# Messages of a graph network as three one-pass matmuls in place of fp32 ones, and h by graphs written by ScalarE and VectorE in place of GpSimd

## The chip, the cores and the metric

The kernel runs on one core of a Trainium2 chip. The metric is the device time of the program in microseconds. The engines of the core (TensorE or PE, VectorE or DVE, ScalarE or ACT, GpSimd or POOL, SyncE or SP) each run their own list of instructions and wait for one another through semaphores.

## The reference

64 graphs of 128 nodes, 128 features per node, all fp32. Each layer input x is normalised and rectified to h; a residual is added at the end.

```python
def _L0_gnn_ref(x, mask, ...):           # x is h here
    xc = jnp.transpose(x, (0, 2, 1))
    h = relu(bn1(conv1d(xc, conv1_w)))                     # 1 tap
    h = bn2(conv1d(h, conv2_w, pad=8))                     # 17 taps
    x_conv = jnp.transpose(relu(h + xc), (0, 2, 1))
    s = x @ w_se.T + b_se                                  # 3 numbers per node
    sq = jnp.sum(s * s, axis=-1)
    dist = sq[:, :, None] + sq[:, None, :] - 2.0 * jnp.einsum('bnd,bmd->bnm', s, s)
    A = jnp.exp(-dist) * mask
    msg = relu(x @ w_msg.T + b_msg)
    x_nmp = jnp.einsum('bnm,bmd->bnd', A, msg)
    gi = concatenate([x_conv, x_nmp], -1) @ w_ih.T + b_ih
    gh = x @ w_hh.T + b_hh
    r = sigmoid(gi_r + gh_r); z = sigmoid(gi_z + gh_z)
    nn_ = tanh(gi_n + r * gh_n)
    return (1.0 - z) * nn_ + z * x
h = jnp.maximum(_layernorm(x, axis=-1), 0.0)
x = x + _L0_gnn_ref(h, adj, ...)
```

The change is about `s` and `msg`: both are products of h with one weight matrix of 132 columns (128 for the messages, 3 for s, one of padding).

## The kernel before

The work goes in 8 groups of 8 graphs (`NG`, `GB`). Features lie on the 128 partitions, and a group's 1024 nodes in two halves of 512 columns (`c` = 0, 1), each in one PSUM bank. In the column order a node comes first and the graph second, so that the 8 graphs of one node are neighbours. Most products are made in three matmuls: a number is split into a high part of type F32R (rounded when written) and the rest as a low part, and `three` (L867 to L870) adds high weights by high data (L868), high weights by low data (L869) and low weights by high data (L870). Two products are fp32 before the change: the messages (L901) and the gather of messages by the affinities (L933). An fp32 matmul stands in the trace as two records of the line.

Per group TensorE runs, in an order written out by hand (L1040 to L1067): nine sub-convolutions (`sub_conv`, matmuls of 256 columns), between them the transposes and distances for the affinities, the gathers, and the transposes of the next group's h (`h_transpose(g + 1, 0, 6)` and `(g + 1, 1, 3)`, into banks 6 and 3); then `gates_h(g, 0)`, `conv1(g + 1)`, `gates_in(g, 0)`, `gates_h(g, 1)`, `messages(g + 1)`, `gates_in(g, 1)`. The gates write banks 3, 4, 5 and 6, so `gates_h(g, 0)` first waits until the next group's h has been read out of banks 6 and 3 (L968).

That reading out: ScalarE writes `h_hi` and `hf`, the high part and the full h (`h_rows`, L402 and L403); VectorE makes `h_lo` from the two (`h_low`, L627); GpSimd copies `hf` into `hg`, where each graph's nodes are together (`by_graphs`, L351), since the messages take a graph's 128 nodes as stationary operand:

```python
pool.tensor_copy(hg[:, :, c * HALF:(c + 1) * HALF],
                 hf[g % 2][:, cols(c)].rearrange("p (n b) -> p b n", b=GB)).then_inc(hg_ready, 1)
```

On VectorE the order around it is also by hand (L836 to L847): `add_shared` (L701), two `join_y` (L709, each waits for one sub-convolution), `n_low` (L729), `h_low(g + 1, 0)`, `add_shared`, `n_low`, `join_y(g, 1, 0)` (waits for sub-convolution 7), `h_low(g + 1, 1)`, `join_y(g, 1, 1)`. ScalarE then makes `xc_hi` (L483) from the finished y, after `ghn_rows` (L489), which reads the first gate matmuls.

`messages(g)` (L891): three F32R matmuls of 396, 396 and 264 columns put the bias in place (L898), then eight fp32 matmuls of 132 columns (L901), one per graph. ScalarE takes s and the messages out (L450 to L457), GpSimd makes the slots for the distances from s (`distances`, L326 to L345).

In the prologue, h and the messages of group 0 are made while the convolution weights are still being split: on ScalarE h_rows stands ahead of the bias row (L535, L536) and the weights' high parts (L385), on VectorE h_low ahead of two weight lots (L620) and the bias row's low part (L807), for which the first messages wait.

Of the kernel before, what the change touches and what calls it, by code (L numbers as in the profile page):

```python
# [10 lines left out]
P = 128  # L11
# [49 lines left out]
def gnn_kernel(nc, x_nm, x_t, adj_t, w_in, w_conv, w_gate, par_in, row_in, out):  # L61
    ctx = ExitStack()
    with ctx:
# [3 lines left out]
        def sem(name):  # L67
# [25 lines left out]

        hg = sb("hg", [P, GB, P])

# [51 lines left out]
            sem("stats_ready"), sem("mv_ready"), sem("pool_ln"), sem("rstd_ready"), sem("hn_ready"))  # L147
        ht_ps, hf_ready, hg_ready, h_lo_ready = (
            sem("ht_ps"), sem("hf_ready"), sem("hg_ready"), sem("h_lo_ready"))

# [109 lines left out]
        def _(pool):  # L260
# [85 lines left out]

            def by_graphs(g, c):
                pool.wait_ge(hf_ready, NCH * g + c + 1)

                upto(pool, msg_ps, g)  # L350
                pool.tensor_copy(hg[:, :, c * HALF:(c + 1) * HALF],  # L351
                                 hf[g % 2][:, cols(c)].rearrange("p (n b) -> p b n", b=GB)).then_inc(hg_ready, 1)

            pool.wait_ge(pool_set, 5)
            ln_scale(0)
            affine()
            by_graphs(0, 0)
            by_graphs(0, 1)
            distances(0)
            for g in range(NG):  # L360
                if g + 1 < NG:
                    ln_scale(g + 1)
                    by_graphs(g + 1, 0)
                    by_graphs(g + 1, 1)
                    distances(g + 1)

        @block.scalar
        def _(act):
# [28 lines left out]
            def h_rows(g, c, src):  # L397
                act.wait_ge(ht_ps, NCH * g + c + 1)

                upto(act, diff_ready, NCH * (g - 2) + c + 1)  # L400
                upto(act, z_ps, NCH * (g - 2) + c + 1)
                act.activation(h_hi[g % 2][:, cols(c)], bank(src), ACT.Relu)  # L402
                act.activation(hf[g % 2][:, cols(c)], bank(src), ACT.Relu).then_inc(hf_ready, 1)  # L403

            def conv1_rows(g, c, src):
# [122 lines left out]

            lot_high(0)
            ln_rows(0)  # L530
            h_rows(0, 0, 6)
# [65 lines left out]
        def _(dve):  # L597
# [25 lines left out]
            def h_low(g, c):  # L623
# [3 lines left out]
                dve.tensor_tensor(h_lo[g % 2][:, cols(c)], hf[g % 2][:, cols(c)], h_hi[g % 2][:, cols(c)],  # L627
                                  ALU.subtract).then_inc(h_lo_ready, 1)

            def level1(g):  # L630
# [164 lines left out]
            moments(0)  # L795
            lot_low(0)
            dve.wait_ge(w2_landed, 16)
            dve.tensor_tensor(fb, w2[:, 0:16:2, :], w2[:, 1:16:2, :], ALU.add).then_inc(sums_ready, 1)
            dve.wait_ge(sums_ready, 1)
            dve.tensor_tensor(fbb, fb[:, 0:8:2, :], fb[:, 1:8:2, :], ALU.add).then_inc(sums_ready, 1)  # L800
            h_low(0, 0)
            h_low(0, 1)
            lot_low(1)
            lot_low(2)
# [17 lines left out]
            for g in range(NG):  # L822
# [17 lines left out]
                if ahead:  # L840
                    h_low(g + 1, 0)
                add_shared(g, 1)
                n_low(g, 1, 7)
                join_y(g, 1, 0)
                if ahead:
                    h_low(g + 1, 1)
                join_y(g, 1, 1)  # L847
                xc_low(g, 0)
# [17 lines left out]
        def _(pe):  # L866
# [24 lines left out]
            def messages(g):  # L891
# [7 lines left out]
                for k, count in enumerate(counts):  # L899
                    for i in range(count):  # L900
                        last = pe.matmul(ps[:, k, i * MW:(i + 1) * MW], hg[:, 3 * k + i, :], w_a[:, P:P + MW],  # L901
                                         start=False, stop=i == count - 1)
                last.then_inc(msg_ps, 1)
# [59 lines left out]
            def gates_h(g, c, ahead):  # L963
                h = (h_hi[g % 2][:, cols(c)], h_lo[g % 2][:, cols(c)])
                if c == 0:

                    if ahead:
                        pe.wait_ge(hf_ready, NCH * (g + 1) + NCH)  # L968
                    else:
                        pe.wait_ge(e_ready, g + 1)  # L970
# [64 lines left out]
            conv1(0, 0, 0)  # L1035
            conv1(0, 1, 7)
            pe.wait_ge(row_split, 3)
            pe.wait_ge(row_ready, 4)
# [78 lines left out]
```

## Time and profile before

| | |
|---|---|
| median of 3 runs | 305.73 us (305.6 to 306.12) |
| profiled execution, its own time | 304.81 us |
| its span (first to last instruction) | 302.8 us |
| instructions | 5350 |
| mean granted clock of TensorE | 0.99 |
| TensorE matmuls (PE) | 279.1 us busy, 92%, 1907 records |
| TensorE weight loads (PEld) | 254.0 us busy, 84%, 1907 records |
| VectorE (DVE) | 230.5 us, 76% |
| ScalarE (ACT) | 179.4 us, 59% |
| GpSimd (POOL) | 90.5 us, 30% |
| L901, messages: matmul records | 128, 15.7 us, mean 276 ns |
| L351, hg by GpSimd | 16, 19.5 us, mean 1219 ns |

A duration is that of one instruction; matmuls overlap in the pipeline, so what a matmul costs is the distance between two starts, not its duration. The chain of waits is followed back from the last instruction, and its pieces don't overlap: a piece is the time that its work held up the end. A wait is put down to the instruction whose semaphore came last. PEclk is the granted clock as a share of 2.4 GHz. L12 is line 12 of the kernel; the changed kernel's lines differ.

### The profile page before, as it was taken

How to read it: one execution, taken by the hardware profiler on the slowest of the kernel's cores; microseconds unless marked ns; L12 is line 12 of the kernel's file. 1: busy time of each engine (PE TensorE's matmuls, PEld its weight loads, DVE VectorE, ACT ScalarE, POOL GpSimd, SP SyncE). 2: the span in 40 equal slices, each digit the busy share in tenths (PEclk: the TensorE clock that was granted, in tenths of full speed). 3: DMA queues.
4: the chain of work that ended last, by engine and by line, in shares of the span. 5: the costliest groups of instructions: out<-in, count | busy, mean ns of one | idle time of the engine just before them, and what ended most of it. 6: DMA issues, size and time to landing. Idle time of an engine off the chain costs nothing.

```text
span 302.8 us, 5350 instructions
## 1 busy us (share of the span) xinstructions
PE 279.1 (92%) x1907; PEld 254.0 (84%) x1907; DVE 230.5 (76%) x477; ACT 179.4 (59%) x342; POOL 90.5 (30%) x159
## 2 busy tenths in 40 slices
PE   0474999999999999999999999999999999999992
PEld 0254998899988998899988998899988998899892
DVE  4489976796787876796787876796787976776446
ACT  2878466657556566656566566556566576561353
POOL 4845330362205530262205520252305520220000
PEclk9998999999999999999999999999999999999998
DMA  7610030017000530017000440007000420022001
GB/s 246 228 47 1 15 128 2 0 31 246 2 3 0 145 135 1 2 19 259 2 0 2 139 141 0 4 13 247 19 0 2 140 71 0 0 61 82 2 0 69
DMA packets 6654, 18.96 MB, mean 63 GB/s; under 512 B 866, under 2 KB 1252, under 8 KB 6500
## 3 DMA queue, kind: packets, MB, share of 16 engines
q1 hardware_dynamic: 6480, 18.62, 19.0%
q8 instruction: 15, 0.25, 0.3%
q14 instruction: 11, 0.09, 0.1%
q10 hardware_dynamic: 148, 0.01, 0.0%
HBM read 14.43 MB, written 4.19 MB: 62 GB/s over the span
## 4 chain that ended last, share of the span: by engine, by line
PE 88%; POOL 3%; DVE 3%; ACT 2%; DMA 2%; issue 1%; SPq 0%; DVEq 0%; POOLq 0%
PE ps L868 25%; PE ps L870 24%; PE ps L869 24%; PE ps L901 5%; PE ps L933 5%; PE ps L877 2%; PE ps L912 1%; PE ps L898 1%; DMA xin<-x_nm 1%; ACT hn L392 1%; PE ps L923 1%; POOL rstd L285 1%; DMA out<-gate 1%; DVE wt_lo L620 0%; POOL sq L329 0%
## 5 line engine op out<-in xcount | busy, mean ns | idle before, releaser
L868 PE MATMUL ps<-v_hi,wt_hi 128*128 128x256 f32 x320 | 93.4, 292 | 1.4 <-DVE wt_lo L620 1.4
L870 PE MATMUL ps<-v_hi,wt_lo 128*128 128x256 f32 x320 | 90.5, 283 | 0.0
L869 PE MATMUL ps<-v_lo,wt_hi 128*128 128x256 f32 x320 | 90.2, 282 | 0.0
L868 PEld LDWEIGHTS ps<-v_hi,wt_hi 128*128 128x128 f32 x320 | 60.8, 190 | 2.6 <-DVE wt_lo L620 1.5
L869 PEld LDWEIGHTS ps<-v_lo,wt_hi 128*128 128x128 f32 x320 | 60.9, 190 | 0.3
L870 PEld LDWEIGHTS ps<-v_hi,wt_lo 128*128 128x128 f32 x320 | 60.6, 189 | 0.0
L392 ACT ACTIVATE hn<-xin,nmr,rstd 128x128 f32<-128x128 f32 x64 | 25.5, 481 | 20.7 <-POOL nmr L287 20.7
L351 POOL COPY hg<-hf 128x512 f32<-128x512 f32 x16 | 19.5, 1219 | 51.1 <-ACT hf L403 51.1
L326 POOL CAST slots<-s_sb 128x48 fp32r<-128x48 f32 x8 | 1.8, 226 | 94.4 <-ACT s_sb L452 94.4
L868 PE MATMUL ps<-h_hi,wt_hi 128*128 128x512 f32 (+1 forms) x67 | 26.8, 400 | 0.7 <-DVE h_lo L627 0.7
L870 PE MATMUL ps<-h_hi,wt_lo 128*128 128x512 f32 (+1 forms) x67 | 26.3, 392 | 0.0
L869 PE MATMUL ps<-h_lo,wt_hi 128*128 128x512 f32 (+1 forms) x67 | 26.2, 392 | 0.0
L701 DVE TENSOR_TENSOR y<-y,mbs 128x512 f32<-128x512 f32 x16 | 11.0, 685 | 17.2 <-ACT mbs L441 17.2
L489 ACT ACTIVATE gn<-ps,par 128x512 f32<-128x512 f32 x15 | 10.3, 688 | 20.0 <-PE ps L870 19.9
L627 DVE TENSOR_TENSOR h_lo<-hf,h_hi 128x512 fp32r<-128x512 f32 x16 | 19.8, 1235 | 3.0 <-ACT hf L403 3.0
L877 PE MATMUL ps<-ident,hn 128*128 128x128 f32 x64 | 10.6, 292 | 10.9 <-ACT hn L392 10.9
L868 PE MATMUL ps<-n_hi,wt_hi 128*128 128x512 f32 (+1 forms) x51 | 20.0, 392 | 0.0
L869 PE MATMUL ps<-xc_lo,wt_hi 128*128 128x512 f32 (+1 forms) x51 | 19.5, 383 | 0.0
L869 PE MATMUL ps<-n_lo,wt_hi 128*128 128x512 f32 (+1 forms) x51 | 19.5, 383 | 0.0
L870 PE MATMUL ps<-n_hi,wt_lo 128*128 128x512 f32 (+1 forms) x51 | 19.5, 382 | 0.0
L870 PE MATMUL ps<-xc_hi,wt_lo 128*128 128x512 f32 (+1 forms) x51 | 19.5, 382 | 0.0
L868 PE MATMUL ps<-xc_hi,wt_hi 128*128 128x512 f32 (+1 forms) x51 | 19.4, 380 | 0.0
(130 smaller groups left out, 636.5 us busy)
## 6 DMA issues: line engine op xcount, KB each, us to landing
mask<-adj_t SPq DMA_DIRECT2D x8, 512.0 KB, 3.5
xt<-x_t SPq DMA_DIRECT2D x8, 512.0 KB, 4.1
out<-gate SPq DMA_DIRECT2D x15, 256.0 KB, 4.1
xin<-x_nm SPq DMA_DIRECT2D x7, 512.0 KB, 3.7
w<-w_conv SPq DMA_DIRECT2D x1, 1088.0 KB, 6.4
gate<-w_gate SPq DMA_DIRECT2D x1, 576.0 KB, 7.4
xin<-x_nm SPq DMA_DIRECT2D x2, 256.0 KB, 2.9
out<-gate SPq DMA_DIRECT2D x2, 128.0 KB, 1.8
```

Of the source, the lines that this page charges most:

```text
L285: pool.tensor_tensor(rstd[:], vpe[:], neg_half[:], ALU.pow).then_inc(pool_ln, 1)
L351: pool.tensor_copy(hg[:, :, c * HALF:(c + 1) * HALF], hf[g % 2][:, cols(c)].rearrange("p (n b) -> p b n", b=GB)).then_inc(hg_ready, 1)
L392: last = act.activation(hn[:, j, :], xin[:, j, :], ACT.Identity, bias=nmr[:, j:j + 1], scale=rstd[:, j:j + 1])
L489: act.activation(gn[c][:], bank(3), ACT.Identity, bias=par[:, HN:HN + 1], scale=0.5).then_inc(ghn_ready, 1)
L627: dve.tensor_tensor(h_lo[g % 2][:, cols(c)], hf[g % 2][:, cols(c)], h_hi[g % 2][:, cols(c)], ALU.subtract).then_inc(h_lo_ready, 1)
L701: dve.tensor_tensor(y_at(s), y_at(s), mbs[1 + s][:].rearrange("p (l b) -> p l b", b=GB).unsqueeze(2).broadcast_to([P, QUART, 2, GB]), ALU. ...
L868: pe.matmul(dst, wt_hi[:, blk, :], hi, start=start, stop=False)
L869: pe.matmul(dst, wt_hi[:, blk, :], lo, start=False, stop=False)
L870: return pe.matmul(dst, wt_lo[:, blk, :], hi, start=False, stop=stop)
L877: last = pe.transpose(ps[:, dst, j * P:(j + 1) * P], hn[:, 4 * c + j, :], ident[:])
L901: last = pe.matmul(ps[:, k, i * MW:(i + 1) * MW], hg[:, 3 * k + i, :], w_a[:, P:P + MW], start=False, stop=i == count - 1)
L933: last = pe.matmul(ps[:, dst, i * P:(i + 1) * P], msg[:, b, :], aff[:, b, :], start=True, stop=True)
```

## The change

The messages are made of F32R parts like the other products. `w_a`'s 132 message columns are split once into `wm_hi` (ScalarE) and `wm_lo` (VectorE). Per half of h, ScalarE writes `hg_hi` by graphs straight from PSUM, as a third copy behind `h_hi` and `hf`, and VectorE writes `hg_lo` from PSUM and `hg_hi` behind `h_low`. GpSimd's `by_graphs` is gone. `messages` has three matmuls of 132 columns per graph. `gates_h(g, 0)` waits for `hg_ready` (both low parts) in place of `hf_ready`.

```diff
--- before.py
+++ after.py
@@ -91,7 +91,10 @@
         h_hi = [sb(f"h_hi{i}", [P, GW], F32R) for i in range(2)]
         h_lo = [sb(f"h_lo{i}", [P, GW], F32R) for i in range(2)]
 
-        hg = sb("hg", [P, GB, P])
+        hg_hi = sb("hg_hi", [P, GB, P], F32R)
+        hg_lo = sb("hg_lo", [P, GB, P], F32R)
+        wm_hi = sb("wm_hi", [P, MW], F32R)
+        wm_lo = sb("wm_lo", [P, MW], F32R)
 
         cp = sb("cp", [P, CPAD, GB])
         u = sb("u", [P, 2, UPAD, GB])
@@ -145,8 +148,8 @@
 
         stats_ready, mv_ready, pool_ln, rstd_ready, hn_ready = (
             sem("stats_ready"), sem("mv_ready"), sem("pool_ln"), sem("rstd_ready"), sem("hn_ready"))
-        ht_ps, hf_ready, hg_ready, h_lo_ready = (
-            sem("ht_ps"), sem("hf_ready"), sem("hg_ready"), sem("h_lo_ready"))
+        ht_ps, hf_ready, hg_hi_ready, hg_ready, h_lo_ready, wm_split = (
+            sem("ht_ps"), sem("hf_ready"), sem("hg_hi_ready"), sem("hg_ready"), sem("h_lo_ready"), sem("wm_split"))
 
         conv1_ps, c_ready, u_ready, vtb_ready, vtu_ready = (
             sem("conv1_ps"), sem("c_ready"), sem("u_ready"), sem("vtb_ready"), sem("vtu_ready"))
@@ -344,24 +347,13 @@
                 pool.wait_ge(pool_s, base + 10)
                 pool.tensor_copy(right[:, :, 14:16], left[:, :, 12:14].bitcast(F32)).then_inc(slots_ready, 1)
 
-            def by_graphs(g, c):
-                pool.wait_ge(hf_ready, NCH * g + c + 1)
-
-                upto(pool, msg_ps, g)
-                pool.tensor_copy(hg[:, :, c * HALF:(c + 1) * HALF],
-                                 hf[g % 2][:, cols(c)].rearrange("p (n b) -> p b n", b=GB)).then_inc(hg_ready, 1)
-
             pool.wait_ge(pool_set, 5)
             ln_scale(0)
             affine()
-            by_graphs(0, 0)
-            by_graphs(0, 1)
             distances(0)
             for g in range(NG):
                 if g + 1 < NG:
                     ln_scale(g + 1)
-                    by_graphs(g + 1, 0)
-                    by_graphs(g + 1, 1)
                     distances(g + 1)
 
         @block.scalar
@@ -402,6 +394,10 @@
                 act.activation(h_hi[g % 2][:, cols(c)], bank(src), ACT.Relu)
                 act.activation(hf[g % 2][:, cols(c)], bank(src), ACT.Relu).then_inc(hf_ready, 1)
 
+                upto(act, msg_ps, g)
+                act.activation(hg_hi[:, :, c * HALF:(c + 1) * HALF], bank(src).rearrange("p (n b) -> p b n", b=GB),
+                               ACT.Relu).then_inc(hg_hi_ready, 1)
+
             def conv1_rows(g, c, src):
                 act.wait_ge(conv1_ps, NCH * g + c + 1)
                 if c == 0:
@@ -527,6 +523,7 @@
                 act.activation(gn[c][:], gn[c][:], ACT.Tanh, bias=par[:, BIN:BIN + 1]).then_inc(cand_ready, 1)
 
             lot_high(0)
+            act.activation(wm_hi[:], w_a[:, P:P + MW], ACT.Copy).then_inc(wm_split, 1)
             ln_rows(0)
             h_rows(0, 0, 6)
             h_rows(0, 1, 3)
@@ -627,6 +624,13 @@
                 dve.tensor_tensor(h_lo[g % 2][:, cols(c)], hf[g % 2][:, cols(c)], h_hi[g % 2][:, cols(c)],
                                   ALU.subtract).then_inc(h_lo_ready, 1)
 
+            def by_graphs_low(g, c, src):
+                dve.wait_ge(hg_hi_ready, NCH * g + c + 1)
+                here = slice(c * HALF, (c + 1) * HALF)
+                dve.scalar_tensor_tensor(out=hg_lo[:, :, here], in0=bank(src).rearrange("p (n b) -> p b n", b=GB),
+                                         scalar=0.0, in1=hg_hi[:, :, here], op0=ALU.max,
+                                         op1=ALU.subtract).then_inc(hg_ready, 1)
+
             def level1(g):
 
                 dve.wait_ge(c_ready, NCH * g + NCH)
@@ -794,12 +798,16 @@
             last.then_inc(stats_ready, 1)
             moments(0)
             lot_low(0)
+            dve.wait_ge(wm_split, 1)
+            dve.tensor_tensor(wm_lo[:], w_a[:, P:P + MW], wm_hi[:], ALU.subtract).then_inc(wm_split, 1)
             dve.wait_ge(w2_landed, 16)
             dve.tensor_tensor(fb, w2[:, 0:16:2, :], w2[:, 1:16:2, :], ALU.add).then_inc(sums_ready, 1)
             dve.wait_ge(sums_ready, 1)
             dve.tensor_tensor(fbb, fb[:, 0:8:2, :], fb[:, 1:8:2, :], ALU.add).then_inc(sums_ready, 1)
             h_low(0, 0)
             h_low(0, 1)
+            by_graphs_low(0, 0, 6)
+            by_graphs_low(0, 1, 3)
             lot_low(1)
             lot_low(2)
             dve.wait_ge(row_split, 2)
@@ -839,11 +847,13 @@
                 n_low(g, 0, 5)
                 if ahead:
                     h_low(g + 1, 0)
+                    by_graphs_low(g + 1, 0, 6)
                 add_shared(g, 1)
                 n_low(g, 1, 7)
                 join_y(g, 1, 0)
                 if ahead:
                     h_low(g + 1, 1)
+                    by_graphs_low(g + 1, 1, 3)
                 join_y(g, 1, 1)
                 xc_low(g, 0)
                 xc_low(g, 1)
@@ -898,8 +908,10 @@
                     pe.matmul(ps[:, k, 0:count * MW], ones[:], row[:, 0:count * MW], start=True, stop=False)
                 for k, count in enumerate(counts):
                     for i in range(count):
-                        last = pe.matmul(ps[:, k, i * MW:(i + 1) * MW], hg[:, 3 * k + i, :], w_a[:, P:P + MW],
-                                         start=False, stop=i == count - 1)
+                        dst, b = ps[:, k, i * MW:(i + 1) * MW], 3 * k + i
+                        pe.matmul(dst, hg_hi[:, b, :], wm_hi[:], start=False, stop=False)
+                        pe.matmul(dst, hg_hi[:, b, :], wm_lo[:], start=False, stop=False)
+                        last = pe.matmul(dst, hg_lo[:, b, :], wm_hi[:], start=False, stop=i == count - 1)
                 last.then_inc(msg_ps, 1)
 
             def factor_transposes(g):
@@ -965,7 +977,7 @@
                 if c == 0:
 
                     if ahead:
-                        pe.wait_ge(hf_ready, NCH * (g + 1) + NCH)
+                        pe.wait_ge(hg_ready, NCH * (g + 1) + NCH)
                     else:
                         pe.wait_ge(e_ready, g + 1)
                     if g == 0:
@@ -1034,6 +1046,7 @@
             pe.wait_ge(wt_lo_ready, 1)
             conv1(0, 0, 0)
             conv1(0, 1, 7)
+            pe.wait_ge(wm_split, 2)
             pe.wait_ge(row_split, 3)
             pe.wait_ge(row_ready, 4)
             messages(0)
```

Three places where instructions moved. VectorE in a group's middle, from the first `n_low` to `xc_low`, before (y is the running sum, L709 joins one sub-convolution to it):

```order
L729 TENSOR_TENSOR n_lo<-ps,n_hi 128x128x4 [waits n_hi_ready]
L627 TENSOR_TENSOR h_lo<-hf,h_hi 128x512 [waits hf_ready]
L701 TENSOR_TENSOR y<-y,mbs 128x64x8 [waits y_ready,mbs_ready]
L729 TENSOR_TENSOR n_lo<-ps,n_hi 128x128x4 [waits n_hi_ready]
L709 SCALAR_TENSOR_TENSOR y<-ps,par,y 128x32x8 [waits y_ready,conv2_ps]
L627 TENSOR_TENSOR h_lo<-hf,h_hi 128x512 [waits hf_ready]
L709 SCALAR_TENSOR_TENSOR y<-ps,par,y 128x32x8 [waits y_ready,conv2_ps]
L716 SCALAR_TENSOR_TENSOR xc_lo<-y,xc_hi 128x512 [waits xc_hi_ready] x2
```

and now:

```order
L733 TENSOR_TENSOR n_lo<-ps,n_hi 128x128x4 [waits n_hi_ready]
L624 TENSOR_TENSOR h_lo<-hf,h_hi 128x512 [waits hf_ready]
L630 SCALAR_TENSOR_TENSOR hg_lo<-ps,hg_hi 128x8x64 [waits hg_hi_ready]
L705 TENSOR_TENSOR y<-y,mbs 128x64x8 [waits y_ready,mbs_ready]
L733 TENSOR_TENSOR n_lo<-ps,n_hi 128x128x4 [waits n_hi_ready]
L713 SCALAR_TENSOR_TENSOR y<-ps,par,y 128x32x8 [waits y_ready,conv2_ps]
L624 TENSOR_TENSOR h_lo<-hf,h_hi 128x512 [waits hf_ready]
L630 SCALAR_TENSOR_TENSOR hg_lo<-ps,hg_hi 128x8x64 [waits hg_hi_ready]
L713 SCALAR_TENSOR_TENSOR y<-ps,par,y 128x32x8 [waits y_ready,conv2_ps]
L720 SCALAR_TENSOR_TENSOR xc_lo<-y,xc_hi 128x512 [waits xc_hi_ready] x2
```

Each `h_lo` has an `hg_lo` behind it, which waits for ScalarE's `hg_hi`; the last `hg_lo` stands behind the join (L713) that waits for sub-convolution 7, and before the last join.

TensorE at the messages of group 1, before (`ones` and `row` are the bias, `n_hi` belongs to the gates that follow):

```order
L870 MATMUL ps<-h_hi,wt_lo 128x512
L898 MATMUL ps<-row,ones 128x396 [waits y_ready,hg_ready,c_ready]
L898 MATMUL ps<-row,ones 128x396
L898 MATMUL ps<-row,ones 128x264
L901 MATMUL ps<-w_a,hg 128x132 x8
L868 MATMUL ps<-n_hi,wt_hi 128x512
```

and now, up to the first graph's three and the start of the second's; the three lines L912 to L914 come eight times:

```order
L880 MATMUL ps<-h_hi,wt_lo 128x512
L908 MATMUL ps<-row,ones 128x396 [waits y_ready,hg_ready,c_ready]
L908 MATMUL ps<-row,ones 128x396
L908 MATMUL ps<-row,ones 128x264
L912 MATMUL ps<-wm_hi,hg_hi 128x132
L913 MATMUL ps<-wm_lo,hg_hi 128x132
L914 MATMUL ps<-wm_hi,hg_lo 128x132
L912 MATMUL ps<-wm_hi,hg_hi 128x132
```

Eight fp32 matmuls have become 24 F32R matmuls at the same place.

VectorE in the prologue, ahead of the bias row's low part for which the first messages wait, before (`gate` holds sums of the convolution weights here):

```order
L800 TENSOR_TENSOR gate<-gate 128x512 [waits sums_ready]
L627 TENSOR_TENSOR h_lo<-hf,h_hi 128x512 [waits hf_ready] x2
L620 TENSOR_TENSOR wt_lo<-w,wt_hi 128x128 [waits wt_hi_ready]
L620 TENSOR_TENSOR wt_lo<-gate,wt_hi 128x512 [waits wt_hi_ready]
L807 TENSOR_TENSOR row<-row_raw,row_hi 1x396 [waits row_landed,row_split]
```

and now:

```order
L806 TENSOR_TENSOR gate<-gate 128x512 [waits sums_ready]
L624 TENSOR_TENSOR h_lo<-hf,h_hi 128x512 [waits hf_ready] x2
L630 SCALAR_TENSOR_TENSOR hg_lo<-ps,hg_hi 128x8x64 [waits hg_hi_ready] x2
L617 TENSOR_TENSOR wt_lo<-w,wt_hi 128x128 [waits wt_hi_ready]
L617 TENSOR_TENSOR wt_lo<-gate,wt_hi 128x512 [waits wt_hi_ready]
L815 TENSOR_TENSOR row<-row_raw,row_hi 1x396 [waits row_landed,row_split]
```

Two `hg_lo` have come between the `h_lo` pair and the weight lots.

## Rows read from the trace of the kernel before

**Rows 1.** The page: busy us (share) of each engine; the chain by engine

```profile
PE 279.1 (92%) x1907; PEld 254.0 (84%) x1907; DVE 230.5 (76%) x477; ACT 179.4 (59%) x342; POOL 90.5 (30%) x159
...
PE 88%; POOL 3%; DVE 3%; ACT 2%; DMA 2%; issue 1%; SPq 0%; DVEq 0%; POOLq 0%
```

**Rows 2.** Windows: us, busy (records) of each engine, clock, DMA

```profile
69.00:103.00 34.00, 34.00 (x236) 31.05 (x235) 27.09 (x57) 21.12 (x40) 10.40 (x18) 1.00 0.19 62
```

**Rows 3.** Chain in order of time, groups 1 and 2: start us, us, what

```profile
72.70 0.89 PE ps L933 x8
...
89.44 0.49 PE ps L898 x3
89.93 1.80 PE ps L901 x16
```

**Rows 4.** Timeline of PE, end of sub-convolutions, start of the gates: start us, us

```profile
77.92 0.28 PE L870 MATMUL ps<-v_hi,wt_lo 128*128 128x256 f32 x1
...
79.35 0.28 PE L870 MATMUL ps<-v_hi,wt_lo 128*128 128x256 f32 x1
79.46 0.40 PE L868 MATMUL ps<-h_hi,wt_hi 128*128 128x512 f32 x1
79.70 0.40 PE L869 MATMUL ps<-h_lo,wt_hi 128*128 128x512 f32 x1
```

**Rows 5.** Groups by line: xcount, busy us, mean ns, idle before

```profile
L869 PEld LDWEIGHTS ps<-v_lo,wt_hi 128*128 128x128 f32 x320 | 60.9, 190 | 0.3
...
L729 DVE TENSOR_TENSOR n_lo<-ps,n_hi 128x512 fp32r<-128x512 f32 x16 | 10.9, 680 | 1.4 <-ACT n_hi L477 1.4
...
L477 ACT ACTIVATE n_hi<-ps 128x512 fp32r<-128x512 f32 x16 | 9.6, 598 | 9.7 <-PE ps L933 9.7
```

**Rows 6.** Timeline of PE and of its weight loads at the distances of group 1

```profile
65.67 0.44 PE L923 MATMUL ps<-rows 16*128 16x128 f32 x8
66.04 0.38 PE L868 MATMUL ps<-v_hi,wt_hi 128*128 128x256 f32 x1
...
66.04 0.19 PEld L868 LDWEIGHTS ps<-v_hi,wt_hi 128*128 128x128 f32 x1
66.15 0.19 PEld L869 LDWEIGHTS ps<-v_lo,wt_hi 128*128 128x128 f32 x1
```

**Rows 7.** Timelines of ACT, POOL and DVE where group 2's h is read out

```profile
77.35 0.60 ACT L403 ACTIVATE hf<-ps 128x512 f32<-128x512 f32 x1
...
78.01 1.21 POOL L351 COPY hg<-hf 128x512 f32<-128x512 f32 x1 [1.64 <-ACT hf L403]
...
78.24 0.48 DVE L709 SCALAR_TENSOR_TENSOR y<-ps,par,y 128x256 f32<-128x256 f32 x1
78.64 1.13 DVE L627 TENSOR_TENSOR h_lo<-hf,h_hi 128x512 fp32r<-128x512 f32 x1
```

**Rows 8.** Line L627, h_low: duration ns min/median/max

```profile
L627 DVE TENSOR_TENSOR h_lo<-hf,h_hi x16: 691/1132/1550, 12.9 to 249.5; 128x512 fp32r<-128x512 f32 x16
```

**Rows 9.** Timelines of ACT, DVE and weight loads in the prologue

```profile
8.75 3.19 ACT L392 ACTIVATE hn<-xin,nmr,rstd 128x128 f32<-128x128 f32 x8 [3.13 <-POOL nmr L287]
...
13.14 0.60 ACT L402 ACTIVATE h_hi<-ps 128x512 fp32r<-128x512 f32 x1 [0.24 <-PE ps L877]
...
14.11 0.52 ACT L535 ACTIVATE row<-row_raw 1x396 fp32r<-1x396 f32 x1
...
8.56 1.24 DVE L798 TENSOR_TENSOR gate<-w 128x1024 f32<-128x1024 f32 x1 [2.46 <-DMA w<-w_conv]
...
14.26 0.89 DVE L627 TENSOR_TENSOR h_lo<-hf,h_hi 128x512 fp32r<-128x512 f32 x1 [0.64 <-ACT hf L403]
15.55 0.73 DVE L620 TENSOR_TENSOR wt_lo<-w,wt_hi 128x128 fp32r<-128x128 f32 x1 [0.40 <-ACT wt_hi L385]
...
16.91 0.56 DVE L807 TENSOR_TENSOR row<-row_raw,row_hi 1x396 fp32r<-1x396 f32 x1
...
17.52 0.48 PEld L898 LDWEIGHTS ps<-row,ones 128*128 128x128 f32 x3 [1.39 <-DVE row L807]
```

## The prediction

> **What bounds the kernel now.** I read the shares first: TensorE shows matmuls for 92% of the 302.8 us, and the chain that ended last runs over TensorE for 88% [rows 1]. In the windows, the stretch from 69 to 103 us (one group of eight graphs takes about 34 us) has PE busy 34.00 of 34.00 us at a granted clock of 1.00, that is 2.4 GHz, while VectorE has 27.1, ScalarE 21.1 and GpSimd 10.4 [rows 2]. So between the prologue and the tail TensorE never stops: whatever lengthens its stream, or makes it wait, lengthens the kernel by as much, and work on the other three counts only where it comes later than TensorE asks for it. Last I took the chain in order of time, where the end of each piece is the start of the next, for what TensorE pays per matmul.
>
> **The messages on TensorE.** Before, eight fp32 matmuls of 132 columns per group show as 16 records and take 1.80 us of the chain [rows 3]: 112.5 ns per record, 225 ns per matmul. Now there are 24 F32R matmuls of 132 columns. What does one take? The trace has F32R with 128 rows at 256 columns (twelve from 77.92 to 79.35: 0.119 us each) and at 512 (0.24 us) [rows 4]. The wide bias matmuls, 396, 396 and 264 columns in 0.49 us [rows 3], give the same slope of 0.46 ns per column. Carried down to 132 columns that is 0.119 - 124 x 0.46 ns = 0.062 us. But every matmul also has a weight load of its own, even where the weights have just been loaded: L868 and L869 use the same wt_hi block, and L869 still has its 320 loads [rows 5]. How long a load takes when nothing covers it stands behind the distances: there the load of L868 starts at 66.04 and the next at 66.15, and the matmul at 66.04 shows 0.38 us where its like shows 0.28 [rows 6, 4]. A load thus costs some 0.10 to 0.11 us. Under a matmul of 256 columns it is hidden; under one of 132 it is not. The narrow neighbours point the same way: the eight records of a gather, 128 columns each, take 0.89 us, 0.111 each [rows 3]. I take 0.112 us, the record of the same width. 24 x 0.112 = 2.69 us against 1.80: +0.89 us per group, +7.1 us over eight. With 0.108 it is +6.3, with 0.118 (no cheaper than 256 columns) +8.3. The lower end, columns alone, is 24 x 0.062 = 1.49 us, or -2.5 us over eight.
>
> The trace has no pair of weight load and narrow F32R matmul at full height, so a rule can be weighed here. The Trainium skill (TensorE: Matmul & The Clock Gate, section Back-to-back issue gap) gives about 81 ns per matmul for a stream of such pairs at 128 columns. By that, 24 of them would take 1.94 us, and the eight groups 1.2 us more instead of 7.1. I keep the row, since no row at 128 or 132 columns and full height is below 0.111.
>
> **The gate matmuls now wait for the by-graph copies.** Before, the first gate matmul of a group waited for ScalarE's second hf half, which was long there: 77.35 + 0.60 = 77.95, for a matmul at 79.46 [rows 4, 7]. Now it waits for hg_ready, since hg_hi and hg_lo read the same PSUM banks, and the second of these comes from VectorE after h_low. VectorE at that place is paced by TensorE: its joining operation L709 starts at 78.24, when sub-convolution 7 has drained (77.92 + 0.28) [rows 4, 7]. Then h_low at 78.64. This one took 1.13 us, because GpSimd's copy ran from 78.01 to 79.22 [rows 7]; without the copy it should take its shortest, 0.69 [rows 8]. Operations on VectorE overlap by 0.08 (78.24 + 0.48 against 78.64), so the next one starts 0.61 after it. The low part then starts at 79.25, and I price it like n_lo, which also reads strided PSUM: 0.68 [rows 5]. It ends at 79.93. ScalarE's hg_hi is no obstacle: it starts behind hf at 77.95 at the latest and takes 0.60, as n_hi does [rows 5]. From VectorE's end to TensorE's weight load I add 0.11 us, and another 0.11 because the load is no longer hidden: 80.15 against 79.46, **0.7 us per group**. It holds in the seven groups that have a group ahead of them: +4.9 us. The bounds: 0.5 us if the low part costs as little as L709's 0.48 [rows 7], 1.15 if it costs 1.13. The h_hi half and the earlier half of the copies have room: on VectorE h_low and the low part together take 0.61 + 0.61 where the blocked h_low took up to 1.55 [rows 8]. What follows on VectorE (L709, 0.2 us later) feeds xc_hi, which stands on ScalarE behind a copy of the gate matmuls that has moved by 0.7 itself.
>
> **The prologue.** TensorE's first messages wait for the bias row's low part on VectorE, which ended 16.91 + 0.56, and the load started at 17.52 [rows 9]. Ahead of it now stand two hg_hi on ScalarE and two low parts on VectorE. ScalarE: two of some 0.5 us, less the 0.24 it waited for the transposes at 13.14, move the row copy from 14.11 to about 14.8. VectorE: the second h_low starts some 0.2 later than 14.26 but takes 0.61 instead of 0.89, so ends as before, near 15.1; two low parts at 0.61 follow, and the next weights start at 16.3 instead of 15.55 [rows 9]: **+0.7 us**. Dearer low parts would make it 1.2. The message weights' own split costs nothing: ScalarE waits 3.13 us for GpSimd then, and VectorE 2.46 us for the convolution weights [rows 9], against about 0.3 us each. If that cover were gone it would be 0.3 us, once.
>
> **GpSimd** loses 16 copies, 19.5 us, none of it on the chain; its distances start when ScalarE has s, which moves with TensorE. That is worth nothing by itself, only what it gives back to h_low, counted above.
>
> **Sum.** 7.1 + 4.9 + 0.7 = +12.7 us. The profiled execution took 304.81 us, so 317.5; the median of the runs, 305.73, is 0.92 above it, so **318.4 us**. A measurement of this kernel can tell about 0.2% (0.6 us) from no change.
>
> **Rivals.**
> - *Columns alone set the rate.* An fp32 record takes nearly twice the column time (0.112 against 0.062), so an fp32 matmul is four passes over its columns; three would then take 1.49 instead of 1.80 us. For it: the slope from 512 to 256 columns and the 1056 columns of bias in 0.49 us [rows 3, 4]. Against it: the bare load of 0.11. -2.5 + 4.9 + 0.7 = +3.1: 308.8 us. The Trainium skill (FP8 and Floating Point Precision, section TensorE Precision Notes) counts true fp32 as four passes; by passes alone, three for four would save a quarter of 1.80 us, 3.6 us in all. A compiler that dropped the second load of hg_hi would come to two loads per graph, 0.22 us, no change in this term, 311.3 us; the 320 loads of L869 speak against it.
> - *Loads half hidden*, somewhere between 0.062 and 0.112 us. Halfway, at 0.087, 24 take 2.09 us: +2.3 + 4.9 + 0.7, 313.6 us. For it speaks only that loads and matmuls do overlap under wide matmuls. The Trainium skill's 81 ns, from the section named above, would make it 312.5 us.
> - *The other side: columns set the rate and the gates don't wait.* It decides at two points: a narrow matmul must cost under 1.80 / 24 = 0.075 us, and h_low and the low part must together end by 79.24, 0.6 us after 78.64. Then -2.5 + 0.7 = -1.8: 303.9 us. Against it stands 1.3 us of VectorE work in that gap of 0.6.
> - *A narrow F32R matmul costs as much as an fp32 one*, 0.225 us: 24 x 0.225 = 5.4, +3.6 per group, +28.8 in all, with the rest 340 us. For it speaks only that no F32R matmul at full height here is narrower than 256 columns. Against it: the eight distance matmuls (F32R, 16 rows, 128 columns) take 0.44 us from the first start to the last end [rows 6], too short for two rounds of 0.22 and a drain.
>
> **Chances.** The forecast 0.72, within 316 (6.3 + 3.5 + 0.5) and 323 (8.3 + 8.0 + 1.2, all at the upper bounds); columns alone 0.10; half hidden 0.06; fp32 price 0.08; the other side 0.04. To hold 8 in 10 the range has to reach down to columns alone: 307 to 323. Faster by over 0.2%: 0.04. Within it: 0.02, for a meeting of the low ends. Slower: 0.94.
>
> **What would show it.** In the changed profile the 24 message records should stand 0.11 us apart, and their piece of the chain near 2.7 us per group. TensorE should wait once in each of groups 0 to 6 at the first gate matmul, 0.5 to 1.1 us, released by the low part on VectorE; L627's successor should show 0.69 everywhere; the first message load should start near 18.2 us. Records 0.06 us apart would make the first term wrong, no wait at the gates the second.

## The result and the profile after

The changed kernel takes 317.56 us (median of 6 runs, 317.4 to 318.46) against 306.07 for the kernel before (6 runs beside it): 1.0369 times, 95% interval 1.0335 to 1.0404. It is slower by some 11.5 us. The forecast was 318.4, within 307 to 323.

The page of the changed kernel (span 315.6 us), shares of the engines and of the chain, against [rows 1]:

```profile
PE 291.0 (92%) x1971; PEld 264.3 (84%) x1971; DVE 232.5 (74%) x494; ACT 186.4 (59%) x359; POOL 62.3 (20%) x143
...
PE 81%; DVE 8%; ACT 5%; issue 2%; POOL 2%; DMA 1%; DVEq 0%; POOLq 0%
```

PE has 64 records more (192 message records in place of 128) and is as dense as before; but 8% of the chain is now VectorE's, where it had 3%. A stretch of one group (columns as in [rows 2]):

```profile
69.50:105.00 35.50, 35.14 (x243) 32.02 (x243) 27.21 (x59) 22.00 (x42) 6.98 (x16) 1.00 0.19 60
```

TensorE is no longer busy throughout: 0.36 us are missing once per group. The distance from one group's first gate matmul to the next group's is 35.73 us (83.48 to 119.21), where it was 34.18 (79.46 to 113.64): +1.55 us. The chain in order of time at the messages of group 2, against [rows 3]:

```profile
93.59 0.49 PE ps L908 x3
94.08 0.06 PE ps L912
94.14 0.11 PE ps L913
94.25 0.11 PE ps L914
94.36 0.11 PE ps L912
...
96.48 0.11 PE ps L913
96.59 0.11 PE ps L914
96.70 0.28 PE ps L878
```

From 94.08 to 96.70 are 2.62 us for 24 records, where 16 took 1.80. Only the first is as short as its columns (0.06 us); each of the others takes 0.11. The gate matmul behind them waits for the rest of its own load, and its piece is 0.28 here and 0.23 before. So from the bias to the second gate matmul it is 3.39 us (0.49 + 2.62 + 0.28) against 2.52 (0.49 + 1.80 + 0.23), and the term is +0.87 us per group.

The end of the reading out of group 2's h, timelines of ScalarE, VectorE, TensorE and its loads, against [rows 4, 7]:

```profile
81.33 0.62 ACT L398 ACTIVATE hg_hi<-ps 128x512 fp32r<-128x512 f32 x1
...
81.74 0.48 DVE L713 SCALAR_TENSOR_TENSOR y<-ps,par,y 128x256 f32<-128x256 f32 x1 [0.51 <-PE ps L880]
82.14 0.68 DVE L624 TENSOR_TENSOR h_lo<-hf,h_hi 128x512 fp32r<-128x512 f32 x1
82.74 0.68 DVE L630 SCALAR_TENSOR_TENSOR hg_lo<-ps,hg_hi 128x512 fp32r<-128x512 f32 x1
...
83.48 0.50 PE L878 MATMUL ps<-h_hi,wt_hi 128*128 128x512 f32 x1 [0.36 <-DVE hg_lo L630]
...
83.48 0.19 PEld L878 LDWEIGHTS ps<-h_hi,wt_hi 128*128 128x128 f32 x1 [0.57 <-DVE hg_lo L630]
83.59 0.19 PEld L879 LDWEIGHTS ps<-h_lo,wt_hi 128*128 128x128 f32 x1
```

hg_lo ends at 83.42 and the gates' first load starts at 83.48. ScalarE had ended at 81.95. So its last copy isn't what the gates wait for. The matmul shows 0.50 us where its like shows 0.40, because its load is bare (not hidden under a matmul), and the matmul behind it starts 0.34 us later where 0.24 is usual. Its own start stands 0.64 us behind that of the matmul before it, 0.12 being usual: 0.52 + 0.10 = 0.62 us per group. GpSimd's copy gone, h_low is at its shortest in every group, against [rows 8]:

```profile
L624 DVE TENSOR_TENSOR h_lo<-hf,h_hi x16: 681/688/693, 12.9 to 260.8; 128x512 fp32r<-128x512 f32 x16
```

The prologue, against [rows 9]: VectorE, loads, GpSimd.

```profile
14.92 1.28 DVE L630 SCALAR_TENSOR_TENSOR hg_lo<-ps,hg_hi 128x512 fp32r<-128x512 f32 x2
16.11 0.28 DVE L617 TENSOR_TENSOR wt_lo<-w,wt_hi 128x128 fp32r<-128x128 f32 x1
...
17.33 0.56 DVE L815 TENSOR_TENSOR row<-row_raw,row_hi 1x396 fp32r<-1x396 f32 x1
...
17.96 0.83 PEld L908 LDWEIGHTS ps<-row,ones 128*128 128x128 f32 x3 [1.98 <-issue]
18.79 0.33 PEld L912 LDWEIGHTS ps<-wm_hi,hg_hi 128*128 128x128 f32 x1
19.01 0.33 PEld L913 LDWEIGHTS ps<-wm_lo,hg_hi 128*128 128x128 f32 x1
...
24.59 0.22 POOL L329 CAST slots<-s_sb 128x48 fp32r<-128x48 f32 x1 [11.86 <-ACT s_sb L448]
...
28.77 0.55 POOL L348 CAST slots<-slots 128x16 fp32r<-128x16 f32 x1
```

The first load of the messages comes 0.44 us later than before. Then something that wasn't forecast: the loads of group 0's messages last 0.33 us and start 0.21 apart, where 0.19 and 0.11 are usual. The kernel before shows the same 0.33 in a stretch where its row of the granted clock reads half speed, 1.2 GHz:

```profile
28.48 0.33 PEld L869 LDWEIGHTS ps<-v_lo,wt_hi 128*128 128x128 f32 x1
...
27.40:30.80 3.40, 3.23 (x15) 3.23 (x16) 3.40 (x8) 3.40 (x7) 0.12 (x1) 0.51 0.01 2
```

But the changed kernel's row for the stretch of these messages reads full speed:

```profile
19.00:24.10 5.10, 5.10 (x25) 5.04 (x24) 4.51 (x7) 0.99 (x2) 0.00 (x0) 1.00 0.00 0
```

The two readings contradict each other. I go by the durations and say that these messages ran at half pace; that it was the clock is inferred, not read from a row. TensorE's convolution and message records in this profile are at half pace from 13.71 us, the first of them, to 28.5.

### The profile page after: what moved, and what is told of

The parts are those of the page before. It is cut to its first block, busy times and chain, and to the rows that moved or that the text cites. A ratio compares the mean times of both kernels' runs of the same rounds, so it can differ in the third digit from the quotient of the medians.

```text
span 315.6 us, 5482 instructions
## 1 busy us (share of the span) xinstructions
PE 291.0 (92%) x1971; PEld 264.3 (84%) x1971; DVE 232.5 (74%) x494; ACT 186.4 (59%) x359; POOL 62.3 (20%) x143
## 4 chain that ended last, share of the span: by engine, by line
PE 81%; DVE 8%; ACT 5%; issue 2%; POOL 2%; DMA 1%; DVEq 0%; POOLq 0%
PE ps L878 22%; PE ps L880 21%; PE ps L879 21%; PE ps L945 4%; PE ps L914 3%; PE ps L913 3%; PE ps L912 2%; ACT hn L384 2%; PE ps L887 2%; DVE h_lo L624 2%; PE ps L908 1%; DVE hg_lo L630 1%; DVE wt_lo L617 1%; POOL rstd L288 1%; DVE stats L596 1%
## 5 line engine op out<-in xcount | busy, mean ns | idle before, releaser
L329 POOL CAST slots<-s_sb 128x48 fp32r<-128x48 f32 x8 | 1.8, 225 | 186.0 <-ACT s_sb L448 186.0
L720 DVE SCALAR_TENSOR_TENSOR xc_lo<-y,xc_hi 128x512 fp32r<-128x512 f32 x16 | 10.4, 689 | 14.9 <-ACT xc_hi L479 14.9
L878 PEld LDWEIGHTS ps<-h_hi,wt_hi 128*128 128x128 f32 x67 | 12.8, 191 | 8.1 <-DVE hg_lo L630 4.0
L713 DVE SCALAR_TENSOR_TENSOR y<-ps,par,y 128x256 f32<-128x256 f32 x32 | 14.8, 480 | 5.8 <-PE ps L880 4.8
```

The costliest lines, as they stand in the source:

```text
L713: dve.scalar_tensor_tensor(out=at, in0=quarter(1 + t), scalar=par[:, SC2:SC2 + 1], in1=at, op0=ALU.mult, op1=ALU.add).then_inc(y_ready, 1)
L720: dve.scalar_tensor_tensor(out=xc_lo[:, cols(c)], in0=y[:, cols(c)], scalar=0.0, in1=xc_hi[:, cols(c)], op0=ALU.max, op1=ALU.subtract).the ...
L878: pe.matmul(dst, wt_hi[:, blk, :], hi, start=start, stop=False)
```

## The experiments

e6 and e10 start from the kernel before, the others from the changed kernel. Times are medians; the ratio is to the kernel before in the same series (305.53 us for e1 to e4, 305.83 for e5 to e7, 305.75 for e8 to e10, 304.81 for e11 and e12).

**e1 and e2: the width of the message matmuls.**

```diff
-pe.matmul(dst, hg_hi[:, b, :], wm_hi[:], start=False, stop=False)
+pe.matmul(dst, hg_hi[:, b, :], wm_hi[:, 0:64], start=False, stop=False)
```

(and likewise the other two, `dst` 64 wide); e2 makes wm_hi, wm_lo and `dst` 200 wide.

> The changed kernel with the moving operand of the 24 message matmuls per group cut from 132 to 64 columns (most of the messages and all of s are then only the bias; the output differs). Theory (the weight load sets the rate of a narrow matmul): records stay 0.11 us apart, the time stays within 0.5 us of the changed kernel's 317.6. Rival (a narrow F32R matmul streams its columns at half rate, two cycles of 2.4 GHz each: 132 columns in 0.110 us): records 0.055 apart, 24 x 0.055 x 8 = 10 us less, about 307.

> The changed kernel with 200 moving columns in place of 132 (operands and places chosen to fit, the messages are other numbers; the output differs). Theory (weight load): 200 columns need about 0.093 us at full rate, still under the load, so records stay 0.11 us apart and the time within 0.5 us of 317.6. Rival (columns at half rate): 0.167 us per record, 24 x 0.057 x 8 = 11 us more, about 328.5.

Measured: 317.54 us (1.04, 1.0378 to 1.0421) and 317.03 us (1.0384, 1.0357 to 1.0411), against 317.56 with 132 columns. Loads at the messages of group 2 with 64 columns, then with 200:

```profile
93.89 0.19 PEld L913 LDWEIGHTS ps<-wm_lo,hg_hi 128*128 128x128 f32 x1
94.00 0.19 PEld L914 LDWEIGHTS ps<-wm_hi,hg_lo 128*128 128x128 f32 x1
...
96.45 0.19 PEld L878 LDWEIGHTS ps<-n_hi,wt_hi 128*128 128x128 f32 x1
```

```profile
93.84 0.19 PEld L914 LDWEIGHTS ps<-wm_lo,hg_hi 128*128 128x128 f32 x1
93.95 0.19 PEld L915 LDWEIGHTS ps<-wm_hi,hg_lo 128*128 128x128 f32 x1
...
96.41 0.19 PEld L878 LDWEIGHTS ps<-n_hi,wt_hi 128*128 128x128 f32 x1
```

The 23 steps from the second message load to the gate load behind take 96.45 - 93.89 = 2.56 us at 64 columns and 96.41 - 93.84 = 2.57 at 200: 0.111 each, with three times the columns. The columns don't set the rate of a matmul this narrow, and half-rate streaming is excluded from both sides. What is left is the weight load: a fixed cost of every matmul would not let the second of the 24 start 0.06 us behind the first. All loads here have 128 columns, so whether 0.11 us is the time of these columns or a fixed cost of any load isn't shown.

**e3: two matmuls per graph in place of three.**

```diff
-pe.matmul(dst, hg_hi[:, b, :], wm_lo[:], start=False, stop=False)
```

> The changed kernel without the product of hg_hi and wm_lo: 16 message matmuls per group in place of 24 (left out: the low part of the message weights). Theory: 8 x 8 records of 0.109 less, 7.0 us less, about 310.6, and the message piece of the chain is again that of the fp32 form, near 1.8 us. Rival (the repeated load of the same hg_hi is nearly free, and the third matmul costs its 0.06 us of columns): 3.9 us less, 313.7.

Measured: 310.96 us (1.017, 1.0137 to 1.0203), 6.6 less. The chain at the messages of group 2:

```profile
92.36 0.48 PE ps L908 x3
92.85 0.06 PE ps L912
...
94.47 0.11 PE ps L913
94.59 0.28 PE ps L878
```

1.74 us for 16 records. So the matmul with the same stationary operand as its neighbour (hg_hi) costs a full load, and two one-pass matmuls cost about what one fp32 matmul did.

**e4 and e11: the wait at the gates, by order on VectorE.**

```diff
-                join_y(g, 1, 0)
                 if ahead:
                     h_low(g + 1, 1)
                     by_graphs_low(g + 1, 1, 3)
+                join_y(g, 1, 0)
```

> The changed kernel, on VectorE h_low and hg_lo of the second half put ahead of the join that waits for sub-convolution 7. Theory (the gates wait because these two stand behind that join): hg_lo ends near 82.8 in group 1's time, TensorE comes at 82.96, so the wait of 0.52 and the bare load of 0.10 go in seven groups: 4.3 us less, 313.3. Rival (the wait is set by ScalarE's third copy, or moves to the joins behind): under 1 us less.

Measured: 313.3 us (1.0264, 1.024 to 1.0288), 4.3 less. VectorE and TensorE in the same place:

```profile
81.27 0.69 DVE L624 TENSOR_TENSOR h_lo<-hf,h_hi 128x512 fp32r<-128x512 f32 x1 [0.26 <-ACT hf L395]
81.87 0.68 DVE L630 SCALAR_TENSOR_TENSOR hg_lo<-ps,hg_hi 128x512 fp32r<-128x512 f32 x1
...
82.61 0.28 PE L880 MATMUL ps<-v_hi,wt_lo 128*128 128x256 f32 x1
82.73 0.39 PE L878 MATMUL ps<-h_hi,wt_hi 128*128 128x512 f32 x1
```

hg_lo ends at 82.55, the gates start 0.12 behind the matmul before them, and the joins behind hold nobody up. Group 0 alone was left with a wait of 0.2. The first gate matmuls of groups 1 and 2 start at 82.73 and 117.81, 35.08 us apart, and the groups up to 6 keep this distance. It is 0.65 under the changed kernel's 35.73 and 0.90 over the 34.18 of the kernel before. This splits the +1.55 per group: 0.65 for the wait, 0.90 for the messages, each 0.03 more than read from the single lines above.

**e5: the same wait, by what is read.**

```diff
-bank(src).rearrange("p (n b) -> p b n", b=GB)
+hf[g % 2][:, cols(c)].rearrange("p (n b) -> p b n", b=GB)
...
-                        pe.wait_ge(hg_ready, NCH * (g + 1) + NCH)
+                        pe.wait_ge(hf_ready, NCH * (g + 1) + NCH)
```

> The changed kernel with hg_hi and hg_lo made from hf in SBUF in place of PSUM, so that the gates wait for hf again and only the messages wait for hg. Theory: the gates' wait goes (0.62 us in seven groups), 4.3 us less, about 313.3, while the message records stay 0.11 apart. Rival (the two extra operations hold VectorE or ScalarE up wherever they stand): under 1 us less.

Measured: 314.36 us (1.0282, 1.0238 to 1.0326), 3.2 less, a miss by 1. In the trace the gates' wait is gone in all seven groups, and the gates of neighbouring groups stand 35.08 us apart as in e4, worth 7 x 0.65 = 4.5 us. But the operations that read hf are longer: in the prologue ScalarE's hg_hi takes 1.14 and 1.16 us where it took 0.58 and 0.59 from PSUM, and VectorE's pair of hg_lo 2.08 where it took 1.28. Counted from the first hn on ScalarE (9.47 us here, 8.69 in the changed kernel), the second gather of group 0 comes 1.4 us later than in the changed kernel. 4.5 - 1.4 = 3.1 meets the 3.2 measured; the longer operations weren't tried alone.

**e8: the same wait, lengthened.**

```diff
                 if ahead:
+                    dve.tensor_tensor(spare[:], mbs[0][0:33, :], mbs[0][0:33, :], ALU.add)
                     h_low(g + 1, 1)
```

> The changed kernel with one more VectorE operation (33 x 256, about 0.35 us to the next one) between the join that waits for sub-convolution 7 and h_low of the second half, in groups 0 to 6. Theory (TensorE's wait is the whole VectorE chain behind that join): 7 x 0.35 = 2.5 us more, about 320.0, and the gap before the gates grows from 0.64 to about 1.0 us. Rival (VectorE has slack there, and the wait is ScalarE's copy or a fixed delay): within 0.5 us.

Measured: 320.27 us (1.0479, 1.0445 to 1.0513), 2.7 more. The waits for hg_lo (total us, times, longest), of the changed kernel and of e8:

```profile
PEld ps L878 <- DVE hg_lo L630: 4.0, 7, 0.6
```

```profile
PEld ps L880 <- DVE hg_lo L631: 6.2, 7, 0.9
```

Seven waits each, longer by 0.31 us. The added operation puts h_low 0.33 us later (83.25 to 83.58), and the gates of neighbouring groups now stand 36.05 us apart, 0.32 more: TensorE pays for VectorE's chain behind the join one for one. That is 2.2 of the 2.7 us; the other 0.5 isn't explained.

**e6: the fp32 messages, hg by ScalarE.** The three matmuls are again one fp32 matmul with w_a; ScalarE's third copy writes an fp32 hg; hg_lo, wm_hi, wm_lo and their operations are left out. Against the kernel before (GpSimd's by_graphs is also gone):

```diff
+                upto(act, msg_ps, g)
+                act.activation(hg[:, :, c * HALF:(c + 1) * HALF], bank(src).rearrange("p (n b) -> p b n", b=GB),
+                               ACT.Relu).then_inc(hg_ready, 1)
...
-                        pe.wait_ge(hf_ready, NCH * (g + 1) + NCH)
+                        pe.wait_ge(hg_ready, NCH * (g + 1) + NCH)
```

> One part of the change alone: messages in fp32 as before, hg written by ScalarE from PSUM as one fp32 copy, no copy on GpSimd, nothing more on VectorE. Theory: no wait at the gates (ScalarE ends 1 us before TensorE comes), h_low always 0.69 us on VectorE, TensorE's stream as before; in the prologue up to 0.6 us later by ScalarE: 305.7 to 306.4. Rival (freeing VectorE of GpSimd's lock gives time back): under 305.

Measured: 307.52 us (1.0042, 1.0008 to 1.0077), 1.3 us over the kernel before by the ratio, and over the 305.7 to 306.4 expected, a miss by 1.1. From group 1 on the two traces keep step: the gates of two neighbouring groups stand 34.17 us apart in both. So it is worth nothing that h_low is no longer lengthened beside GpSimd's copy. What is left lies in the prologue, where this profile has group 0's messages at half pace (16 records in 3.2 us of loads) and then 6.8 us in which the granted clock is 0.50; neither was tried alone:

```profile
28.10:34.90 6.80, 5.16 (x28) 4.82 (x29) 5.41 (x22) 3.46 (x8) 3.02 (x6) 0.50 0.01 1
```

**e7: matmuls that keep TensorE busy ahead of the first messages.**

```diff
+            for _ in range(5):
+                pe.matmul(bank(5), wt_hi[:, CONV1, :], h_hi[0][:, cols(1)], start=True, stop=True)
             pe.wait_ge(wm_split, 2)
```

> The changed kernel with five extra matmuls of 512 columns between conv1 of group 0 and its messages, into a bank that nothing reads before it is written anew, in a stretch where TensorE was idle for 1.9 us. Theory (the first messages ran at 1.2 GHz because of that gap, 0.21 us a record): the records stand 0.11 apart, messages end 2.5 us earlier, but GpSimd's distances meet VectorE's weight lots again, so 0.5 to 2.5 us less. Rival (the clock stays low whatever is done there, or the prologue is set by other engines): within 0.3 us.

Measured: 317.91 us (1.0399, 1.0358 to 1.044): nothing gained, against 0.5 to 2.5 us less expected. The first messages did run at full pace (records 0.11 apart from 19.70 on), but GpSimd's part of the distances took 7.6 us in place of 5.1 (s at 22.53, last slot done at 30.13; 24.27 and 29.32 in the changed kernel). TensorE stood idle for 4.3 us before the distances, where it had been 0.4, and behind that the granted clock was 0.50:

```profile
28.60:35.40 6.80, 5.22 (x28) 4.89 (x29) 5.95 (x23) 4.01 (x9) 2.42 (x6) 0.50 0.01 2
```

That the extra matmuls brought the full pace isn't shown. e8 has the changed kernel's prologue without them, and the loads of its first messages last 0.19 us, full pace too; e9 and e12 below also have both paces without them. e8 shows as well what full pace is worth in the new form: counted from the first hn on ScalarE, the second gather of group 0 starts after 34.65 us in e7 and in e8, and after 34.37 in the changed kernel, whose messages ran at half pace. It gains nothing.

**e9 and e12, e10: group 0 in the other form.** e9 is e4 with GpSimd's copy and fp32 messages in group 0; e10 is the kernel before with the new form in group 0 alone.

```diff
+                        if g == 0:
+                            last = pe.matmul(dst, hg[:, b, :], w_a[:, P:P + MW], start=False, stop=i == count - 1)
+                            continue
```

> As e4 (no wait at the gates), and group 0 as in the kernel before: hg copied by GpSimd (into memory of aff, still unused), fp32 messages. Theory: what is left of the change is the message term of seven groups, 7 x 0.89 = 6.2 us over the kernel before, about 312.0, and 1.3 us or more under e4. Rival (the prologue is set by the distances on GpSimd, whatever the form of group 0's messages): no difference from e4's 313.3.

> The kernel before with group 0 alone in the new form (hg_hi by ScalarE, hg_lo by VectorE, 24 message matmuls; memory of n_hi and n_lo, still unused). Theory: it bears the prologue's share by itself, as the difference between the two profiles has it: 1.5 to 2.0 us more than the kernel before, about 307.8. Rival (it is given back while TensorE waits for the distances): within 0.3 us of the kernel before.

Measured: e9 313.9 us (1.0261, 1.0226 to 1.0297; single runs from 311.91 to 314.6), e10 307.26 us (1.0052, 1.0033 to 1.0071). e10 bears the prologue's share by itself, 1.6 us, as expected. e9 went by its rival: no time under e4, though the span of its profile (309.8) was 1.7 us shorter. So both were run again on one chip:

> The kernel of e4 once more, beside e12 on one chip. Both theories: 313.3, 1.026 times the kernel before.

> The kernel of e9 once more, beside e11 on one chip, since its runs spread from 311.9 to 314.6 and its profile (span 309.8) is 1.7 us shorter than e4's (311.5). Theory (group 0's form costs in the prologue): 1.0 to 2.0 us under e11. Rival (what the prologue gains is mostly given back, by TensorE's clock and the distances): within 0.6 us of e11.

Measured: e11 313.3 us (1.027, 1.0239 to 1.0301), e12 313.03 us (1.0259, 1.0216 to 1.0303; runs from 311.96 to 315.48). Two profiles of this one program, group 0's fp32 messages in e9 and in e12:

```profile
18.46 1.96 PE L925 MATMUL ps<-w_a,aff 128*128 128x132 f32 x16
```

```profile
19.58 3.73 PE L925 MATMUL ps<-w_a,aff 128*128 128x132 f32 x16
```

The same 16 records take 1.96 us in one execution and 3.73 in the other: full pace in one, half pace in the other, though the row of the granted clock reads 1.00 over both. At the second gather of group 0, e9 stands 0.63 us behind the kernel before and e12 2.06; e4, with the new form in group 0, 2.10, and e11, the same program as e4, 2.78. Part of this is only a later start: ScalarE's first hn comes at 8.75 us in the kernel before, 8.85 in e4, 9.08 in e9, 9.51 in e11 and 9.74 in e12. Counted from there, the new form stands 2.0 us behind the kernel before in four profiles (the changed kernel, e4, e10, e11), the old form 0.3 in e9 and 1.1 in e12. The profiles thus give the new form 0.9 to 1.7 us in the prologue, but the medians only 0.3 (e12 under e11) or nothing (e9 against e4). Its size in the full kernel stays unsettled between 0 and 2 us.

## Why the prediction was right

**The messages.** Forecast 24 x 0.112 = 2.69 us against 1.80, +0.89 per group; measured 2.62 for the piece, +0.87 with the gate matmul behind it, and +0.90 by the distance between groups in e4. The reason given, a bare weight load of 0.10 to 0.11, is what e1, e2 and e3 show: width does not matter from 64 to 200 columns, and each record left out gives back 6.6 us / 64 = 0.103. The rivals of columns alone (308.8), of loads half hidden (0.087 us a record, 313.6) and of an fp32 price (340) fall, as does the other side (303.9), since both its conditions fail. So does the 81 ns per pair of the Trainium skill ("TensorE: Matmul & The Clock Gate", back-to-back issue gap): here a pair takes 0.111 us.

**The wait at the gates.** Forecast 0.7 us in seven groups, +4.9; measured 0.62 to 0.65, some +4.5, and e4 gives back 4.3, which is 4.5 less the 0.2 that group 0 still waits. Place, releaser and count were as forecast. The term was a little too large in one piece: from VectorE's end to the load I had 0.11 us, and it was 0.06 (83.42 to 83.48). The part that wasn't sure, 0.68 for hg_lo, came out at 0.68. The bounds of 0.5 and 1.15 held it. e8, which lengthens the chain behind the join, and e4 and e5, which take it away by two means, leave no other cause for this term.

**The prologue.** Forecast +0.7, with group 0's messages +1.6; the profile has +1.95 at the second gather of group 0, e10 gives 1.6 by the clock of whole runs. The sum is near, the working was not, and that it came near is luck. The first message load came 0.44 later, not 0.7: L617, the operation behind the low parts, started at 16.11, not 16.3, and took 0.28 in place of 0.73. Group 0's messages, which I had at the pace of the kernel before, ran at half that pace and took 5.1 us, so that s came 4.16 us later (20.11, now 24.27). More than half of that came back, which I hadn't seen either: GpSimd's part of the distances took 5.1 us (last slot at 29.32) where it had taken 7.4, and it began while VectorE stood idle between weight lots (23.80 to 26.05). TensorE's half pace up to 28.5 ended before the last slot was there, so it cost nothing after the messages. From there on 0.17 came back up to the first gather, and 0.32 was lost before the second, where TensorE waited for ScalarE's mbs. The upper bound of this term was also too low in itself: two low parts at the 1.13 us of the dearer case come to 1.6, not 1.2.

**The sum.** 7 x 0.90 + 7 x 0.65 + 1.95 = 12.8 us, the difference of the two spans (315.6 - 302.8); the forecast was 12.7. So close a meeting is partly luck: the wait came out 0.35 us under its term and the prologue with group 0's messages 0.35 over. The medians differ by 11.5 only, because the profiled execution of the kernel before, from which the sum was made, was 1.3 us quicker than the median of 306.07. GpSimd's 16 copies were worth nothing on the chain, as said (e6).

## What to carry to other kernels

Count weight loads, not passes: where a matmul of TensorE streams its columns in less time than its load takes (here some 0.11 us for a load of 128 columns, by the slope as long as 240 columns of data; measured alike at 64, 132 and 200), splitting fp32 into three one-pass matmuls replaces two records by three and loses. When a new operation is put between a producer and the release of its PSUM bank, look at what its engine waits for just ahead of it: here a join paced by TensorE stood there, so every microsecond behind it was TensorE's, and putting the reading-out ahead of the join (e4) took the wait away and cost nothing elsewhere. The dearer messages remain: e4 is still 2.6% slower than the kernel before.

## What the runs showed of the hardware that was not expected

- The same program ran its first fp32 messages at full pace in one execution and at half pace in another (16 records in 1.96 and 3.73 us, e9 and e12). Counted from the same point, the second gather then came 0.77 us later, less than the 1.77 us of difference: GpSimd's part of the distances took 8.0 us in e9 and 6.3 in e12. In the new form the same difference of pace (e8 and the changed kernel) moved the second gather by -0.28 us.
- The row of the granted clock can read 1.00 over a stretch in which TensorE's records have the durations of half speed (19.00 to 24.10 us of the changed kernel: loads of 0.33 us, elsewhere 0.19).
- GpSimd's small operations of the distances took 5.1 us in the changed kernel, where VectorE was idle during the first six of them (0.20 to 0.28 us each) and busy during the last five (0.52 to 0.75), and 7.4 us beside VectorE's weight lots in the kernel before. One and the same operation (sq, L332 now, L329 before) took 0.20 and 1.06.
- The same copy by graphs on ScalarE takes 0.62 us reading PSUM (hg_hi, median of 16) and 1.16 reading SBUF (e5, median of 16). It is Relu in one and Copy in the other, so the place alone isn't shown to be the cause.
- The first narrow matmul behind the wide ones costs only its columns: the second starts 0.06 us after it. One load more than its own can then have been hidden under the wide ones; from the third on each waits for its load.
